# A two-part layer on one core: the second part's hidden layer as seven products of half matrices

## The reference

```python
x = x + mamba(layernorm(x))                       # state of 512 x 16 per token, a scan over the tokens
y = layernorm(x)
h = silu((y @ w1.T) * s1) * ((y @ w2.T) * s2)     # 256 -> 1024
h = gelu((h @ h1.T) * t1)                         # 1024 -> 1024
h = gelu((h @ h2.T) * t2)                         # 1024 -> 1024, the layer that the change touches
x = x + (h @ w3.T) * s3                           # 1024 -> 256
```

## Time and profile before

| | us |
|---|---|
| median of three runs | 2768.11 (2767.78 to 2770.92) |
| the profiled execution | 2766.63 |
| its span, which the profile shows | 2764.8 |
| TensorE busy | 2587.6 (94%) |
| VectorE busy | 2249.4 (81%) |
| ScalarE busy | 1970.6 (71%) |
| GpSimd busy | 1770.2 (64%) |

### The profile page before, as it was taken

The page is one execution under the profiler, slowest core; times in us unless marked ns, Lnnn a source line. Parts: engine busy times, 40 slices in busy tenths (PEclk is TensorE's granted clock), DMA queues, the critical chain, the costliest instruction groups (busy, mean ns, idle before and its releaser), DMA issues.

```text
span 2764.8 us, 48560 instructions
## 1 busy us (share of the span) xinstructions
PE 2587.6 (94%) x17026; PEld 2290.3 (83%) x17026; DVE 2249.4 (81%) x2891; ACT 1970.6 (71%) x4136; POOL 1770.2 (64%) x1547
## 2 busy tenths in 40 slices
PE   6679999999999999999999999999979899999998
PEld 5558888888888888888888888888868788888887
DVE  4999999999999999999999999999982255554444
ACT  7898888888888888888888888888875222222221
POOL 3788888888888888888888888888872000000000
PEclk8899999999999999999999999999989999999999
DMA  6112112112112121121121122221231322222221
GB/s 232 43 46 71 59 60 69 58 59 66 59 62 70 62 74 62 59 70 58 59 66 59 62 67 62 73 67 59 62 115 66 122 92 80 73 92 77 92 62 32
DMA packets 130151, 198.74 MB, mean 72 GB/s; under 512 B 16368, under 2 KB 93296, under 8 KB 129904
## 3 DMA queue, kind: packets, MB, share of 16 engines
q1 hardware_dynamic: 129904, 195.57, 22.0%
HBM read 144.68 MB, written 50.86 MB: 71 GB/s over the span
## 4 chain that ended last, share of the span: by engine, by line
PE 65%; DVE 18%; issue 9%; ACT 6%; DVEq 0%; DMA 0%; POOL 0%; SPq 0%; ACTq 0%; POOLq 0%
PE banks L1434 17%; PE banks L1469 16%; PE banks L1446 10%; DVE h L1151 9%; PE banks L1346 7%; DVE acc L1164 5%; PE banks L1492 4%; PE banks L1397 4%; DVE silu L1136 3%; PE banks L1420 2%; PE banks L1357 2%; ACT banks L1022 2%; PE banks L1388 1%; PE banks L1410 0%; ACT ssm L804 0%
## 5 line engine op out<-in xcount | busy, mean ns | idle before, releaser
L1151 DVE TENSOR_TENSOR_SCAN h<-banks,ub 128x512 f32<-128x512 f32 x1024 | 1196.4, 1205 | 40.5 <-ACT banks L1022 33.7
L763 POOL TENSOR_TENSOR ub<-u,b_row 128x1020 f32<-128x1020 f32 x512 | 1214.2, 2371 | 0.3 <-issue 0.2
L1164 DVE SCALAR_TENSOR_TENSOR acc<-banks,c_tok,acc 128x512 f32<-128x512 f32 x1024 | 717.6, 735 | 76.7 <-PE banks L1446 76.6
L1022 ACT ACTIVATE banks<-dt,neg_a 128x510 f32<-128x510 f32 x1024 | 698.7, 687 | 68.7 <-DVE h L1151 67.7
L1446 PE MATMUL banks<-ident,h 128*128 128x128 f32 x4096 | 598.6, 278 | 100.3 <-DVE acc L1164 63.0
L1446 PEld LDWEIGHTS banks<-ident,h 128*128 128x128 f32 x4096 | 479.2, 142 | 189.3 <-DVE h L1151 109.2
L1434 PE MATMUL banks<-act_high,h_rounded 128*128 128x256 f32 x2048 | 512.9, 291 | 4.3 <-POOL act_low L790 3.0
L1434 PE MATMUL banks<-act_low,h_rounded 128*128 128x256 f32 x2048 | 492.9, 280 | 0.0
L1469 PE MATMUL banks<-act_high,h_rounded 128*128 128x512 f32 x1024 | 400.2, 391 | 13.2 <-DVE act_low L1213 13.2
L1469 PE MATMUL banks<-act_low,h_rounded 128*128 128x512 f32 x1024 | 400.0, 391 | 0.0
L1434 PEld LDWEIGHTS banks<-act_high,h_rounded 128*128 128x128 f32 x2048 | 387.5, 189 | 10.7 <-issue 10.0
(11 more groups left out here) (119 smaller groups left out, 4006.7 us busy)
## 6 DMA issues: line engine op xcount, KB each, us to landing
b_row<-b_scratch SPq DMA_DIRECT2D x128, 512.0 KB, 4.0
z_scratch<-z_out SPq DMA_DIRECT2D x128, 256.0 KB, 2.1
zl<-z_scratch SPq DMA_DIRECT2D x32, 1024.0 KB, 8.1
x_sb<-in_x SPq DMA_DIRECT2D x32, 256.0 KB, 4.3
x_res<-in_x SPq DMA_DIRECT2D x32, 256.0 KB, 3.4
h_full<-in_h SPq DMA_DIRECT2D x2, 4096.0 KB, 17.9
x_scratch<-x_sb SPq DMA_DIRECT2D x32, 256.0 KB, 2.9
xr<-x_scratch SPq DMA_DIRECT2D x16, 512.0 KB, 4.8
```

Source lines behind the costliest of these rows:

```text
L763: nc.gpsimd.tensor_tensor(ub[:, n % 2, :, 1:], u[:, :, 1:], b_row[:, n // QUARTER % 2, n % QUARTER:n % QUARTER + 1, 1:].to_broadcast([P, E ...
L1022: nc.scalar.activation(decay_half(k)[:, :, 1:], dt[:, par, 2 * i:2 * i + 2, 1:], ACT.Exp, scale=neg_a[:, n:n + 1]).then_inc(decay_ready, 1)
L1151: nc.vector.tensor_tensor_scan(h[:, n % 2, 2 * i:2 * i + 2].rearrange("p e t -> p (e t)"), banks[:, k % DECAYS, :], ub[:, n % 2, 2 * i:2 * ...
L1164: nc.vector.scalar_tensor_tensor(out=acc[:, par, q], in0=turned[q], scalar=c_tok[:, par, q, n:n + 1], in1=acc[:, par, q], op0=ALU.mult, op ...
```

## The change

**The product.** The layer's result C (1024 outputs x 512 tokens) is cut into four quarters, Cij with output half i and token half j; so are the activations X (Aij: input half i, token half j) and the weights (`h11`, `h12`, `h21`, `h22` in the code: h12 takes input half 2 to output half 1, h21 input half 1 to output half 2). In place of eight products of quarters there are seven, by Winograd's form of Strassen's scheme:

- sums of the activations, per block: T1 = A12 - A11, T2 = A22 - T1, T4 = A21 - T2, T3 = A22 - A12 (GpSimd, `t_of`, 128 x 1024 each)
- sums of the weights, once: S3 = h11 - h21, S1 = h21 + h22, S2 = S1 - h11, S4 = h12 - S2 (GpSimd in the tail, `sum_of`; ScalarE checks that they are exact and rounds them, `sum_piece`)
- products, each in two halves of 16 matmuls of 256 columns (`product`): A11·h11, A21·h12, T2·S2, T3·S3, T4·h22, T1·S1, A22·S4
- sums of the products on VectorE, from PSUM (`take_product`): `u_odd` = A11·h11 (ScalarE, `product_out`), C11 = A21·h12 + u_odd, `u_even` = T2·S2 + u_odd, `u_odd` = T3·S3 + u_even, C21 = T4·h22 + u_odd, `u_even` = T1·S1 + u_even, C22 = T1·S1 + u_odd, C12 = A22·S4 + u_even

**The splits.** All high parts of the inputs are now rounded by ScalarE (`high_a_rows`, `high_rows`), the low parts of A11 and A21 are taken by VectorE (`split_rows`), those of T2, T3, T4, T1 and A22 by GpSimd (`low_rows`). The second gelu works in SBUF on quarters (`gelu_quad`), ScalarE rounds its result, VectorE takes the low part (`split_quad`).

**The order of TensorE in a block**: A11, A21, T2, then w3 of the block before, then T3, T4, T1, A22.

**The tail.** The rows of block 1 are loaded at step (CHUNKS + 1, 15). In the tail stand five half products of block 0 (A11, A21 and half of T2) in place of four whole jobs, the sums of the weights and of block 0's activations on GpSimd, and their checks and roundings on ScalarE. The check ends, and the flag is made, at the end of chunk CHUNKS + 2 of the tail instead of in chunk 1. The residual is loaded straight into `out_e`; the last block is stored in two halves.

```diff
-        W3_AFTER = 3
-        FIRST_ROWS = [(CHUNKS, 20) for o in range(KH)]
-        IN_TAIL = {(CHUNKS, 30): (0,), (CHUNKS + 1, 6): (1,), (CHUNKS + 2, 6): (2, 3)}
+        BEFORE_W3 = ("A11", "A21", "T2")
+        AFTER_W3 = ("T3", "T4", "T1", "A22")
+        IN_TAIL = {(CHUNKS + 2, 6): (("A11", 0), ("A11", 1)), (CHUNKS + 2, 19): (("A21", 0), ("A21", 1)),
+                   (CHUNKS + 2, 22): (("T2", 0),)}
+        SUM_AT = {(CHUNKS + 1, 9): (("S3", 0), ("S3", 1)), (CHUNKS + 1, 13): (("S1", 0),), (CHUNKS + 1, 16): (("S1", 1),),
+                  (CHUNKS + 2, 9): (("S2", 0), ("S2", 1)), (CHUNKS + 2, 16): (("S4", 0),), (CHUNKS + 2, 21): (("S4", 1),)}
...
+            def second_rows(c, n):
+                if (c, n) == (CHUNKS + 1, NS - 1):
+                    wait_full(sp, f"h{PAIRS - 1}", CHUNKS - 2)
+                    load_z(1)
...
-                    if blk + 3 < CB:
-                        sp.wait_ge(e_full, e_place["h2", blk, KH - 1] + 1)
-                        load_z(blk + 3)
+                    if blk + 2 < CB:
+                        e_done(sp, ("A22", blk, 1))
+                        load_z(blk + 2)
...
+            def t_of(name, blk):
...
+                first, second = {"T1": ("A12", "A11"), "T2": ("A22", "T1"), "T4": ("A21", "T2"), "T3": ("A22", "A12")}[name]
+                nc.gpsimd.tensor_tensor(raw_of(name, blk), raw_of(first, blk), raw_of(second, blk), ALU.subtract).then_inc(t_ready, 1)
+
+            def low_rows(name, blk):
...
+                nc.gpsimd.tensor_tensor(low_of(name, blk), raw_of(name, blk), t_high[name][:].bitcast(F32), ALU.subtract).then_inc(low_t, 1)
...
+            def exact():
+                pass_a_over(pool)
+                for blk in range(CB):
+                    low_rows("A22", blk)
+                    if blk + 1 < CB:
+                        for name in T_ORDER:
+                            t_of(name, blk + 1)
+                        for name in LOW_ORDER[:4]:
+                            low_rows(name, blk + 1)
...
+            def gelu_quad(blk, name):
+                for half in range(2):
...
+                    for i in range(2):
+                        o = KQ * (int(name[1]) - 1) + 2 * half + i
+                        last = nc.scalar.activation(rows[:, 2 * half + i], rows[:, 2 * half + i], ACT.Gelu, scale=scales[:, 3, o:o + 1])
...
+                    nc.scalar.activation(act2_half(act2_high, name, half), rows[:, 2 * half:2 * half + 2], ACT.Copy).then_inc(high2_ready, 1)
...
+                    if blk + 1 < CB:
+                        first(blk + 1)
+                        high_a_rows("A11", blk + 1)
+                        high_a_rows("A21", blk + 1)
+                    gelu_quad(blk, "C11")
+                    if blk + 1 < CB:
+                        for name in LOW_ORDER[:3]:
+                            high_rows(name, blk + 1)
+                    gelu_quad(blk, "C21")
...
+            def product(blk, name, half):
+                into = free((name, blk, half))
+                if name in ("A11", "A21"):
+                    pe.wait_ge(split_a, 2 * blk + ("A11", "A21").index(name) + 1)
+                else:
+                    wait_low(pe, name, blk)
+                high, low = t_high[name], low_of(name, blk)
+                for i in range(2):
+                    for k in range(KQ):
+                        for rows in (high, low):
+                            last = nc.tensor.matmul(into[:, i * T:(i + 1) * T], weights_of(name, k, 2 * half + i), rows[:, k],
+                                                    start=(k == 0 and rows is high), stop=(k == KQ - 1 and rows is low))
```

More of the change, by code:

```diff
@@ L522, in on_flag @@
                 exact()
-            with eng.Else():
-                general()
+            if general is not None:
+                with eng.Else():
+                    general()
         block = ctx.enter_context(nc.Block())
@@ L797, in _ @@
+            ending(post, mlp, NS, in_tail)
+            def exact():
[7 more added lines that the diff above has]
+                            low_rows(name, blk + 1)
+            on_flag(pool, exact, None)
         @block.scalar
@@ L1057, in _ @@
+                for name, half in SUM_AT.get((c, n), ()):
+                    wait_full(act, "out", CHUNKS - 1)
+                    sum_piece(name, half)
+                if (c, n) == (CHUNKS + 2, 9):
+                    wait_full(act, f"gg{PAIRS - 1}", CHUNKS - 1)
+                    high_rows("T2", 0)
             ending(post, mlp, ACT_STEPS, first_rows)
             def exact():
-                def second(blk, o):
-                    row = KH * blk + o
-                    job = ("h2", blk, o)
-                    after(act, split2, row - WIDE + 1)
-                    act.wait_ge(e_full, e_place[job] + 1)
-                    nc.scalar.activation(wide[:, row % WIDE], e_bank(job), ACT.Gelu, scale=scales[:, 3, o:o + 1]).then_inc(e_free[e_place[job] % E_RING], 1)
+                def gelu_quad(blk, name):
+                    for half in range(2):
+                        e_taken(act, ({"C11": "A21", "C21": "T4", "C22": "T1", "C12": "A22"}[name], blk, half))
+                        rows = quad[:, QUADS.index(name) % 2]
+                        for i in range(2):
+                            o = KQ * (int(name[1]) - 1) + 2 * half + i
+                            last = nc.scalar.activation(rows[:, 2 * half + i], rows[:, 2 * half + i], ACT.Gelu, scale=scales[:, 3, o:o + 1])
+                        last.then_inc(gelu2_ready, 1)
+                        if name == "C11" and half == 0 and blk >= 1:
+                            e_done(act, ("out", blk - 1, NTB // 2 - 1))
+                        act.wait_ge(gelu2_ready, place2(name, blk, half))
+                        nc.scalar.activation(act2_half(act2_high, name, half), rows[:, 2 * half:2 * half + 2], ACT.Copy).then_inc(high2_ready, 1)
@@ L1252, in exact @@
+                last_quad(CB - 1)
                 finish(CB - 1)
@@ L1478, in in_tail @@
                             pe.wait_ge(y_added[q], NS * CHUNKS)
-                    second_layer(0, o)
+                    if (name, half) == ("T2", 0):
+                        pe.wait_ge(sums_rounded, SUMS)
+                    product(0, name, half)
+                if (c, n) == (FLAG_CHUNK, FLAG_AT):
+                    into = wait_bank("flag", 0)
+                    pe.wait_ge(flag_step, FLAG_STEPS)
+                    nc.tensor.matmul(into[0:1, 0:1], not_exact[:], ones[:], start=True, stop=True).then_inc(job_full, 1)
             ending(post, mlp, PE_STEPS, in_tail)
```

435 lines of the change are left out of this document (318 added, 117 removed).

## The result

| | before | after |
|---|---|---|
| median of the runs, us | 2768.27 (4 runs) | 2730.68 (2730.3 to 2731.1, 4 runs) |
| span of the profiled execution, us | 2764.8 | 2729.4 |
| the profiled execution, us | 2766.63 | 2731.1 |

The ratio is 0.9862, with a 95% interval of 0.9845 to 0.9879: 37.6 us faster. The forecast was 2725 us in a range of 2709 to 2752.

A forecast was written before the change was run, and what follows sets the result against it. TensorE was taken as the bound: 2193.6 us to block 1, 2.3 slow clock, 14 blocks of 34.2, then 33.8 + 7.7 + 0.3 + 1.3 + 4.2 give a 2722.0 us span; with 1.8 and 1.5 added, 2725.3, range 2709 to 2752.

The forecast's parts named there:

- Products at 116.8 ns, 26.16 us: Second part: 224 matmuls of 256 columns per block at h1's spacing, 2.90 us less than the 29.06 us of wide ones.
- Turns cost TensorE 1.2 us every second or third block, 34.2 a block: Steady blocks: VectorE's two-SBUF-input instructions take turns with GpSimd, raising a block from 33.83 to 34.2 us.
- Rival A: Second part: turns cost nothing, block 1 starts at 2189.0, blocks take 33.83 us, 2715.5 us in all; chance 0.24.
- lengthening on GpSimd instead of VectorE: Sign against the forecast: in the turns, GpSimd's instructions grow longer rather than VectorE's 512 splits, expected towards 1.5 us.
- waits of 0.1, 2.4, 2.4, 2.1, 2.1 = 9.1: VectorE's queue from w3's end, in turns with GpSimd: done at 38.7 us, 1.1 to 1.2 late for A21 at 37.6.
- rival B: Steady blocks: GpSimd served first, VectorE waits; 38.0 us a block, 2786 us in all, 0.6% slower; chance 0.08.
- ScalarE 25.4, VectorE 19.8, GpSimd 21.5 us a block without turns: Second part: the other engines' work per block, none reaching TensorE's 33.8 us, so hand-overs decide.
- Block 1 at 2193.6: Tail: block 1 starts once VectorE has split A11 at 2193.5, only 1.6 us before the earlier kernel's 2195.2.
- The estimate of 1.3 us for the flag: Tail: 1x1 matmul, its cast and the flag's fetch behind A21, so other engines enter the second part about 2167.2.
- The end: Behind the last block's w3: about 0.3 us waiting, 1.3 on VectorE, 4.2 from the store's issue to the span's end.
- The sum: Whole span: block 1's start, slow clock, 14 blocks, last block and end add to 2722.0 us against 2764.8, -42.8.
- C: Rival: tail or hand-overs 5 to 15 us later, or products spaced 119.9 ns (+10); about 2736 us in all; chance 0.15.

The follow-up runs named there:

- rows32: Changed kernel with unused pads of 32 to 128 bytes, meant to begin moving operands 32 bytes past stationary ones in the second part: 2716.45 us, ratio 0.9816.
- pool_more: Changed kernel with four more two-input 128x512 additions on GpSimd in every block, result untouched: 2732.18 us, ratio 0.9871.
- rows192: Changed kernel with pads that put every moving operand of the second part 192 bytes past its stationary one, modulo 256: 2713.08 us, ratio 0.9808.
- a11_first: Changed kernel with VectorE's split of block 1's A11 moved ahead of block 0's C11 sums: 2729.61 us, ratio 0.9865.
- late_load: Changed kernel without its early load: block 1's rows loaded behind the last chunk's stores, once the flag is known: 2734.83 us, ratio 0.9882.
- splits_first: Changed kernel with VectorE's splits of both A11 and A21 of block 1 moved ahead of block 0's C11 sums: 2726.98 us, ratio 0.9856.
- rows0: Control: changed kernel with all tiles moved together by 64 bytes, operand distances unchanged: 2730.63 us, measured once.
- rows64: Changed kernel with the pads of rows32 resized for a distance of 64 bytes, some operands at 192 modulo 256: 2715.26 us, ratio 0.9813.
- mixed: Changed kernel padded as in rows192, but with product T2 at 96, T4 at 128 and T1 at 224 bytes: 2711.38 us, measured once.
- before_rows32: Kernel before the change, with pads meant for a distance of 32 bytes in its second part: 2775.55 us, ratio 1.0033.
- best: Changed kernel with the moves of splits_first and the pads of rows192, the first part's layers also at 192 bytes: 2709.82 us, ratio 0.9793.

## Why the prediction was right, and where it was not

**Mechanism right, by the trace.** TensorE stayed the bound, the gain is the shorter block, and the start of block 1 hangs on VectorE's split of A11. Step by step:

- *Products at 116.8 ns, 26.16 us*: 120.0 and 26.88. This is the term that was mis-sized. The prediction had both numbers, took h1's spacing as the nearest kin by form, and w3's 119.9 as the bound. The right kin was w3: not by form but by where its operands lay (distance 0). rows32 comes within 0.5 ns of the forecast's value by moving tiles alone. The wrong term costs 0.72 us a block.
- *Turns cost TensorE 1.2 us every second or third block, 34.2 a block*: they cost nothing; TensorE has no wait in the steady blocks, not even at 33.75 us (rows32) or with some 5 us more of GpSimd's work (pool_more). Rival A's half of the story was the right one. The two errors nearly cancel, 34.56 against 34.2, and that is luck.
- *The turns themselves* are there. Groups of VectorE and GpSimd in the changed kernel, 2250 to 2700 us:

```profile
L1487 DVE TENSOR_TENSOR act_low<-quad,act_high 128x512 fp32r<-128x512 f32 x104 | 129.9, 1280 | 23.3 <-ACT act_high L1291 23.3
L1474 DVE TENSOR_TENSOR quad<-banks,u_odd 128x512 f32<-128x512 f32 x78 | 50.8, 679 | 0.0
L1457 DVE TENSOR_TENSOR zl_low<-zl_raw,A_high 128x1024 fp32r<-128x1024 f32 x26 | 38.5, 1482 | 0.0
```

```profile
L938 POOL TENSOR_TENSOR T_low<-T_raw,T_high 128x1024 fp32r<-128x1024 f32 x39 | 117.2, 3006 | 27.1 <-ACT T_high L1246 25.9
L933 POOL TENSOR_TENSOR T_raw<-zl_raw,T_raw 128x1024 f32<-128x1024 f32 x25 | 60.3, 2410 | 3.3
```

  Splits of 512 take 1.28 us on average where the earlier trace rows has 0.69; additions with one input in PSUM keep 0.68, as forecast. What was not forecast is that GpSimd pays too (3.01 against 2.40). The prediction named lengthening on GpSimd instead of VectorE as a sign against itself; it is both.
- *Why the turns didn't reach TensorE.* The step that failed is the count of "waits of 0.1, 2.4, 2.4, 2.1, 2.1 = 9.1". One steady block, GpSimd and then VectorE (start, length, and the idle time before):

```profile
2423.13 2.42 POOL L933 TENSOR_TENSOR zl_raw<-zl_raw 128x1024 f32<-128x1024 f32 x1
2426.67 2.83 POOL L938 TENSOR_TENSOR T_low<-T_raw,T_high 128x1024 fp32r<-128x1024 f32 x1 [1.12 <-ACT T_high L1246]
2429.46 2.88 POOL L938 TENSOR_TENSOR zl_low<-zl_raw,T_high 128x1024 fp32r<-128x1024 f32 x1
2432.40 3.45 POOL L938 TENSOR_TENSOR T_low<-T_raw,T_high 128x1024 fp32r<-128x1024 f32 x1
2436.29 3.46 POOL L938 TENSOR_TENSOR T_low<-T_raw,T_high 128x1024 fp32r<-128x1024 f32 x1 [0.44 <-ACT T_high L1246]
```

```profile
2424.32 2.32 DVE L1491 TENSOR_TENSOR out_e<-prod_e,out_e 128x1024 f32<-128x1024 f32 x1
2426.56 3.49 DVE L1487 TENSOR_TENSOR act_low<-quad,act_high 128x512 fp32r<-128x512 f32 x2
...
2432.36 1.21 DVE L1457 TENSOR_TENSOR zl_low<-zl_raw,A_high 128x1024 fp32r<-128x1024 f32 x1
...
2436.26 1.22 DVE L1457 TENSOR_TENSOR zl_low<-zl_raw,A_high 128x1024 fp32r<-128x1024 f32 x1
```

  GpSimd's row has holes where it waits for ScalarE's high parts; ScalarE in its turn had waited for TensorE, 2.6 us for w3 and 2.8 for a product. VectorE lost 1.1 us at the sum and 2.2 at two splits, 3.3 in all. The splits of A11 and A21, which TensorE needs, lost nothing: each started 0.03 to 0.04 us ahead of a GpSimd instruction, which then took 3.45 instead of 2.40. A21's split ended at 2437.48; TensorE asks for it when A11's product is done, at 2442.7. That leaves 5.2 us, where the forecast had it 1.1 late.

  This is the common case but not the only one. In another block A11's split started behind GpSimd, and waited:

```profile
2398.84 2.41 POOL L938 TENSOR_TENSOR T_low<-T_raw,T_high 128x1024 fp32r<-128x1024 f32 x1
```

```profile
2398.92 3.41 DVE L1457 TENSOR_TENSOR zl_low<-zl_raw,A_high 128x1024 fp32r<-128x1024 f32 x1
2404.65 1.36 DVE L1457 TENSOR_TENSOR zl_low<-zl_raw,A_high 128x1024 fp32r<-128x1024 f32 x1
```

  VectorE lost 6.7 us there. That happened in 4 of the 14 steady blocks. The most that VectorE lost in any of them was 6.8 us against the 9.1 of the forecast, and the slow matmuls gave it 0.8 us more (A21 is asked for 38.4 us into a block of 34.56, not 37.6). So A11's split was always in time, by 1.7 us at the least and by 5.2 at the most. In rows32, at 33.75 us a block, the least is 1.0; in rows192, at 32.95, it is 0.2, at the very place where the rhythm changed.

  In these rows whoever starts first is served, and the other waits until that instruction has ended: A11's split, 0.08 us behind GpSimd, took 3.41 us (1.21 where it doesn't wait), and GpSimd, 0.04 us behind a split, took 3.45 (2.40). The rows also show who comes next when both queues are full: VectorE's second split waited out one GpSimd instruction, until 2429.5, and then got in ahead of the next, which took 2.88. So VectorE never waited out GpSimd's run, as rival B had it.
- *ScalarE 25.4, VectorE 19.8, GpSimd 21.5 us a block without turns*: ScalarE 24.8 (143.38 of 200 us), VectorE 24.5 and GpSimd 23.7 with turns in them. ScalarE's gelus of 256 were taken at 0.44 and are 0.45 apart (0.90 for two). (VectorE's terms add up to 20.25. The 0.45 that the prediction took off is the overlap of nine neighbours at 0.05, and there are 27 instructions; nothing hangs on it.)
- *Block 1 at 2193.6*: 2194.41. The last chunk's layer and A21 ended 3.2 us later than forecast (2169.1 against 2165.9), since h1's stretch from 2119.85 took 17.45 us instead of 14.95: the granted clock is 0.87 there, where the kernel before has 1.00 from 2122 to 2137. The change itself seems to have brought this about: the two jobs that it took away had kept TensorE busy from 2115 to 2120, where it is now busy for 0.78 us of 5, and behind that hole the clock is 0.54 from 2120 to 2125 (0.50 in the first half of it), where the kernel before has 1.00. The holes ahead of block 1 speak for the same cause: behind 5.1 us (a11_first), 5.8 (changed kernel), 11.0 (late_load) and 13.2 (kernel before) the clock is 0.50; in splits_first, where no wait is longer than 1.6 us, it is 1.00 from 2186 to 2250. The prediction counted the jobs' time as saved and the clock at nothing. The engines behind it made up for most of that: C11's splits ended at 2188.6 (2187.5 forecast), A11's at 2194.3 (2193.5). (The terms that the prediction gives for ScalarE's work add up to 2183.9 and not to its 2184.3.) The estimate of 1.3 us for the flag is near the trace: from A21's end, 2169.1, to ScalarE's first rounding behind the flag, 2170.3, it took 1.2 us. The slow clock behind the hole cost 2.5 us (21.73 for 160 matmuls that take 19.20 at 120 ns), the forecast had 2.3. The windows of the changed kernel, h1's stretch and the start of block 1 (columns as in the earlier trace rows; the two lines from 2115 to 2125 show TensorE alone):

```profile
2120.00:2137.00 17.00, 17.00 (x127) 17.00 (x128) 0.78 (x1) 9.99 (x15) 6.28 (x3) 0.87 0.13 47
```

```profile
2115.00:2120.00 5.00, 0.78 (x5) 0.78 0.00 0
2120.00:2125.00 5.00, 5.00 (x26) 0.54 0.01 3
```

```profile
2194.00:2199.00 5.00, 4.59 (x21) 4.62 (x22) 5.00 (x6) 3.90 (x8) 4.85 (x2) 0.50 0.57 182
```

- *The end*: 6.4 us behind w3 instead of 5.8.
- *The sum*: 0.8 (block 1) + 0.2 (clock) + 14 x 0.36 (5.0) + 0.8 (last block) + 0.6 (end) = 7.4, which is 2729.4 - 2722.0.
- *C* had the spacing of 119.9 as one of its causes at 0.15; that cause came true alone, without the late tail.

## What to carry to other kernels

Take a matmul's price from the trace, but from the kin whose operands lie alike in SBUF, not only from the one of the same shape; and where TensorE is the bound, try a few pads of 32 to 192 bytes between moving and stationary tiles, width by width: here they gave 14 to 18 us of 2730 with no change of the work. Turns between VectorE and GpSimd are to be counted only against the instruction that the bound engine asks for, with GpSimd's own waits in its row; 3 to 7 us of turns in a block were free because 1.7 us of slack or more was left where they mattered. Read the slack over all blocks and not in one, and again after each gain: the shorter block of rows192 had used it up. Where one wait is taken away, price what was queued behind it: an early load that ended an 8 us wait was worth 4.

## What was not expected of the hardware

- The spacing of matmuls with 256 columns in fp32r, in turn with their weight loads and at full granted clock, changed with how far apart the moving and the stationary operand begin, modulo 256 bytes. A distance of 0 gives 120.0 ns in every block of the changed kernel, rows0, a11_first and late_load. The others, by product: 32 gives 116.5 to 117.8 (rows32), 64 gives 116.6 to 117.8 (rows64; A22 113.3 in every second block), 96 gives 119.6 and 128 gives 120.1 (mixed, one product each), 160 gives 117.2 to 119.0 (rows32), 192 gives 113.3 or 117.8 (rows192, rows64), 224 gives 118.3 (mixed, one product). With 512 columns 0 gives 227.0, and a mixture of 32 and 160 gives 230 to 235 (before_rows32).
- At one distance, 192 bytes, the products held two rhythms, each for over 100 us: in rows192 113.4 ns from 2214.7 to 2331.7 and 117.8 from there to the end. In rows192 and in best they changed in the middle of a block, where VectorE's split came so late that TensorE was delayed by 0.05 us (159 ns in place of 113) and by 0.16 us (198 and 192 ns); products and w3 changed in opposite directions. In rows64 they take turns from block to block. That the delay is the cause isn't shown. One attempt to pick the rhythm by w3's own distance failed.
- The smallest spacing that a whole product of 256 columns showed here is 113.3 ns, at a granted clock of 1.00 (rows64, rows192, mixed).
- A GpSimd instruction can lose the turn as well as VectorE: 3.45 us instead of 2.40 when VectorE's split had started 0.04 us before it.
